# Minus mu enters the second attention's sigmoid through three more rows of the score product, not through ScalarE's bias operand

## What is computed

```
scores = jnp.einsum('bhqd,bhkd->bhqk', q, k) / scale
scores = jax.nn.sigmoid(scores - mu) * jnp.exp(scores)
scores = scores / jnp.sum(scores, axis=-1, keepdims=True)
out = jnp.einsum('bhqk,bhkd->bhqd', scores, v)
```

## Time and profile before

| what | value |
|---|---|
| median of 3 runs | 779.44 us (777.09, 779.44, 789.72) |
| profiled execution, first to last instruction | 779.1 us |
| PE busy | 707.4 us (91%) |
| DVE busy | 442.6 us (57%) |
| ACT busy | 357.8 us (46%) |
| POOL busy | 129.2 us (17%) |

### The profile page before, as it was taken

The page is one execution under the profiler, slowest core; times in us unless marked ns, Lnnn a source line. Parts: engine busy times, 40 slices in busy tenths (PEclk is TensorE's granted clock), DMA queues, the critical chain, the costliest instruction groups (busy, mean ns, idle before and its releaser), DMA issues.

```text
span 779.1 us, 16167 instructions
## 1 busy us (share of the span) xinstructions
PE 707.4 (91%) x5688; PEld 580.0 (74%) x5696; DVE 442.6 (57%) x1125; ACT 357.8 (46%) x610; POOL 129.2 (17%) x166
## 2 busy tenths in 40 slices
PE   5687999999989999999999999998899999998635
PEld 4466878878768999999999999996566665665423
DVE  3557688888673342344222232332788898866666
ACT  3242454345533212122212112213998989988435
POOL 2010122232132210000001001002634222210000
PEclk9699999999999999999999999999999999999855
DMA  6979166355737566555555555571875447651002
GB/s 172 213 133 262 31 97 102 79 86 87 121 109 268 189 209 223 189 192 172 180 189 181 199 192 177 169 180 46 101 113 95 67 63 104 82 65 18 1 14 95
DMA packets 70839, 102.54 MB, mean 132 GB/s; under 512 B 8416, under 2 KB 58600, under 8 KB 70640
## 3 DMA queue, kind: packets, MB, share of 16 engines
q1 hardware_dynamic: 67376, 93.15, 50.7%
q0 software_dynamic: 3136, 8.40, 4.2%
q10 hardware_dynamic: 256, 0.07, 0.0%
HBM read 63.75 MB, written 12.58 MB: 98 GB/s over the span
## 4 chain that ended last, share of the span: by engine, by line
PE 61%; DVE 17%; ACT 7%; DMA 7%; issue 5%; POOL 1%; SPq 1%; ACTq 1%; DVEq 0%; POOLq 0%
PE psum L1981 18%; PE psum L2032 17%; DVE arena L1304 9%; DMA arena<-arena 5%; PE psum L1661 4%; PE psum L1924 3%; PE psum L1685 2%; PE psum L1930 2%; ACT arena L830 2%; PE psum L1939 1%; POOL w0T L699 1%; PE psum L2009 1%; DVE arena L1157 1%; PE psum L2149 1%; PE psum L1654 1%
## 5 line engine op out<-in xcount | busy, mean ns | idle before, releaser
L1981 PEld LDWEIGHTS psum<-arena 128*128 128x128 f32 x1248 | 144.9, 192 | 2.1 <-issue 0.3
L1981 PE MATMUL psum<-arena 128*128 128x128 f32 x1248 | 146.1, 275 | 0.1
L2032 PE MATMUL psum<-arena 128*128 x624 | 141.4, 380 | 0.8 <-DVE arena L1450 0.8
L859 ACT ACTIVATE arena<-psum,arena 128x128 f32<-128x128 f32 x156 | 44.5, 368 | 194.7 <-PE psum L1981 115.2
L2032 PEld LDWEIGHTS psum<-arena 128*128 128x128 f32 x624 | 115.5, 190 | 15.4 <-issue 1.2
L1432 DVE TENSOR_SCALAR arena<-psum,arena 128x128 f32<-128x128 f32 x156 | 44.0, 345 | 80.5 <-PE psum L1981 67.3
L1939 PE MATMUL psum<-arena 96*128 96x256 bf16 x512 | 75.1, 274 | 9.1 <-ACT arena L829 5.7
L1304 DVE TENSOR_TENSOR arena<-arena 128x1024 f32<-128x1024 f32 x64 | 79.9, 1316 | 4.5 <-ACT arena L829 2.6
L1939 PEld LDWEIGHTS psum<-arena 96*128 96x128 bf16 x512 | 44.3, 97 | 44.0 <-ACT arena L829 14.4
L699 POOL DMA_INDIRECT w0T<-yg,pos x32 | 37.4, 1169 | 222.6 <-DMA yg<-arena 176.2
L1450 DVE TENSOR_TENSOR arena<-psum,arena 128x256 f32<-128x256 f32 x39 | 16.6, 425 | 96.6 <-PE psum L2032 96.6
(11 more groups left out here) (290 smaller groups left out, 1207.8 us busy)
## 6 DMA issues: line engine op xcount, KB each, us to landing
arena<-in_L_ffn_w_dram SPq DMA_DIRECT2D x47, 1024.0 KB, 5.1
arena<-arena SPq DMA_DIRECT2D x192, 128.0 KB, 5.1
arena<-xg SPq DMA_DIRECT2D x39, 128.0 KB, 2.0
yg<-arena SPq DMA_DIRECT2D x39, 128.0 KB, 1.7
out_dram<-arena SPq DMA_DIRECT2D x8, 256.0 KB, 2.1
xg<-zeros SPq DMA_DIRECT2D x9, 128.0 KB, 2.9
arena<-in_x_dram SPq DMA_DIRECT2D x8, 128.0 KB, 3.1
arena<-in_L_ffn_b_dram SPq DMA_DIRECT2D x1, 1024.0 KB, 14.9
```

The costliest lines, as they stand in the source:

```text
L859: ins = act.activation(hidT[:, v, c, :], psum[:, 2 * v, c * P:(c + 1) * P], ACT.Relu, bias=b1c[:, v, c:c + 1])
L1981: mm = pe.matmul(psum[:, 2 * v + c // HALF, (c % HALF) * P:(c % HALF + 1) * P], w1b[:, i % W1_BUFS, d, c * P:(c + 1) * P], xtT[:, v, d, :] ...
L2032: mm = pe.matmul(y_bank, hidT[:, u, c, :], w2s[:, one(e), c, :].rearrange("p o n -> p (o n)"), start=(c == 0), stop=(c == HC - 1))
```

## The change

The sigmoid loses its bias operand. In its place the score product of the sigmoid's pass contracts over 99 rows (`MU_ROWS`): rows 96 to 98 of `stackq1` hold ones, the same rows of `stackk1` hold minus mu, split into three bf16 parts whose sum is the fp32 value. The exp's pass still contracts over 96 rows. To fill those rows:

- DVE splits `neg_mu` and sets each part in its partition, with seven instructions on 128 x 1 values, behind the output of MoE tile 7 (`mu_parts`).
- POOL writes ones and then minus mu's parts into partitions 96 to 127 of the first copies, two instructions on 32 x 4096 bf16 values, once the first layer of MoE tile 9 is done.
- SP copies the three rows to the second copies with two DMAs of 24 KB each after the last tile is stored (`mu_rows_copied`); PE waits for them before batch 1.

```diff
-                    return act.activation(out, in_, ACT.Sigmoid, bias=neg_mu[:])
+                    return act.activation(out, in_, ACT.Sigmoid)
...
-                def scores(b, u, p, done):
+                def scores(b, u, p, done, rows):
...
-                                           stackk1[u][0:ROWS, hd, kt * P:(kt + 1) * P], stackq1[u][0:ROWS, hd, :],
+                                           stackk1[u][0:rows, hd, kt * P:(kt + 1) * P], stackq1[u][0:rows, hd, :],
...
+                                pe.wait_ge(S["consts"], ROW_CONSTS + 2)
+                            if b == 1 and p == 0:
+                                pe.wait_ge(S["w_in"], LATE_LOADS + 2 * 16)
...
-                            scores(b, u, p, S["s1_mm"])
+                            scores(b, u, p, S["s1_mm"], (ROWS, MU_ROWS)[u])
...
-                            scores(b, u, p, S["s2_mm"])
+                            scores(b, u, p, S["s2_mm"], (ROWS, MU_ROWS)[v])
...
+                pool.wait_ge(S["l1_hi"], EARLY_TILES + 2)
+                pool.memset(stackq1[0][ROWS:P], 1.0).then_inc(S["consts"], 1)
+                pool.wait_ge(S["consts"], ROW_CONSTS + 1)
+                pool.wait_ge(S["p_const"], MU_STEPS)
+                pool.tensor_scalar(stackk1[0][ROWS:P], stackq1[0][ROWS:P], mu_r[ROWS:P, 2:3], None, ALU.mult
+                                   ).then_inc(S["consts"], 1)
+                pool.wait_ge(S["consts"], ROW_CONSTS + 2)
...
+                def mu_rows_copied():
+
+                    sp.wait_ge(S["l2_mm"], MOE_TILES)
+                    sp.wait_ge(S["y_ev"], MOE_TILES)
+                    for u in range(2):
+                        sp.wait_ge(y_st[u], 16 * ((MOE_TILES + 1 - u) // 2))
+                    sp.wait_ge(S["consts"], ROW_CONSTS + 2)
+                    for stack in (stackq1, stackk1):
+                        sp.dma_start(stack[1][ROWS:MU_ROWS], stack[0][ROWS:MU_ROWS]).then_inc(S["w_in"], 16)
...
+                    if i == 7:
+                        mu_parts()
```

More of the change, by code:

```diff
@@ L67 @@
 SHIFT_ROW = ROWS
+MU_PARTS = 3
+MU_ROWS = ROWS + MU_PARTS
 Q_SLOTS = ((0, 1, 2), (3, 4), (5,))
@@ L124, in tower_kernel @@
         neg_mu = sb("neg_mu", [P, 1], F32)
+        mu_p = sb("mu_p", [P, 2], BF16)
+        mu_r = sb("mu_r", [P, 3], F32)
         ones_row = sb("ones_row", [1, P], F32)
@@ L399, in tower_kernel @@
         WT_STEPS = 10
+        CONST_STEPS = 7
+        MU_STEPS = CONST_STEPS + 7
+        ROW_CONSTS = 15
         PLAN_STEPS = 22
@@ L596, in _ @@
                 moe_tiles(tile)
+                def mu_rows_copied():
[6 more added lines that the diff above has]
+                        sp.dma_start(stack[1][ROWS:MU_ROWS], stack[0][ROWS:MU_ROWS]).then_inc(S["w_in"], 16)
                 def iteration(b, u, k):
+                    if b == 0:
+                        mu_rows_copied()
                     if stages(b + 1, 0, LAST):
@@ L1420, in weight_rounded, with mu_link, mu_parts @@
                     assert steps[0] == W8_STEPS
+                mu_steps = [CONST_STEPS]
+                def mu_link(ins):
+                    mu_steps[0] += 1
+                    ins.then_inc(S["p_const"], 1)
+                    dve.wait_ge(S["p_const"], mu_steps[0])
+                def mu_parts():
+                    dve.wait_ge(S["wT_done"], WT_STEPS + 3)
+                    mu_link(dve.tensor_copy(mu_p[:, 0:1], neg_mu[:]))
+                    mu_link(dve.tensor_tensor(mu_r[:, 0:1], neg_mu[:], mu_p[:, 0:1], ALU.subtract))
+                    mu_link(dve.tensor_copy(mu_p[:, 1:2], mu_r[:, 0:1]))
+                    mu_link(dve.tensor_tensor(mu_r[:, 1:2], mu_r[:, 0:1], mu_p[:, 1:2], ALU.subtract))
+                    mu_link(dve.tensor_tensor(mu_r[:, 2:3], mu_p[:, 0:1], ident[:, ROWS:ROWS + 1], ALU.mult))
+                    mu_link(dve.scalar_tensor_tensor(out=mu_r[:, 2:3], in0=mu_p[:, 1:2], scalar=ident[:, ROWS + 1:ROWS + 2],
+                                                     in1=mu_r[:, 2:3], op0=ALU.mult, op1=ALU.add))
+                    mu_link(dve.scalar_tensor_tensor(out=mu_r[:, 2:3], in0=mu_r[:, 1:2], scalar=ident[:, ROWS + 2:ROWS + 3],
+                                                     in1=mu_r[:, 2:3], op0=ALU.mult, op1=ALU.add))
+                    assert mu_steps[0] == MU_STEPS
                 def tile(i, u):
```

## The result

| | median | lowest to highest | runs |
|---|---|---|---|
| before | 782.39 us | 777.09 to 789.72 | 6 |
| after | 793.94 us | 787.72 to 794.98 | 6 |

The ratio is 1.0116 with an interval of 1.0082 to 1.0151, so the change costs 9.1 us (6.4 to 11.8) of 782.4. The two medians of the table stand further apart, 11.6 us or 1.48%; the text goes by the ratio, which has the interval. The forecast was 0.7 us less, 778.7 us with a range of 775.6 to 781.4, made on the 779.44 us of the three runs of before that were known then. The profiled execution of the changed kernel took 794.69 us, its span 792.9.

The account below looks back on a forecast made before the run. The second attention was taken as bound by a chain of waits through DVE's multiplications, PE and ACT, with one sigmoid per batch on it. 8 x 0.09 = 0.72 us saved, other parts 0, gave 778.7 us, range 775.6 to 781.4.

Parts of the forecast that it names:

- Two POOL instructions of 32 x 4096: MoE stage near 317 us: memset 5 us and multiplication 7 us, covered by over 100 us; cost 0 unless DVE suffers.
- third rival: MoE stage: POOL's long instructions hold DVE, which holds PE beyond 3 us slack; 783.4 us, at most 790; chance 0.05.
- The bias operand: Second attention: dropping it saves 0.09 us per sigmoid, one per batch on the path, 0.72 us in all.
- eight-fold sum of 0.7 us: Second attention: 8 x 0.09 = 0.72 us saved, one sigmoid on the path in each batch.
- The 99 rows: Second attention's score matmuls: three more rows cost 0; with scatter, 0.2 us in all either way.
- The seven DVE instructions: Behind MoE tile 7's output: cost 0, covered by PE's matmuls; without that cover at most 2.8 us.
- SP's copies and PE's waits: Copies in SP's 8.9 us gap before the spread at 543.74 us, waits covered: cost 0, at most 1.3 us.
- fourth rival: End of second attention, 730 to 745 us: PE's clock steps at another moment, 3 us either way, 776 or 782; chance 0.08.

Follow-up runs that it names:

- f2: Changed kernel with POOL's long multiplication left as it was and DVE's copy of b1 written as a maximum over a one-element axis: 787.13 us, ratio 0.999 to before.
- e4: Kernel before with the sigmoid's bias operand dropped and nothing in its place, minus mu left out of the computation: 787.28 us, ratio 1.0009 to before.
- e1: Changed kernel with POOL's multiplication made by one ACT instruction at tile 9, POOL keeping the memset: 786.93 us, ratio 1.0013 to before.
- e2: Changed kernel with POOL's multiplication split into 16 instructions of 32 x 256, one per head: 789.27 us, ratio 1.0023 to before.
- f4: Changed kernel with POOL's multiplication split into two instructions of 32 x 2048: 787.84 us, ratio 1.0013 to before.
- e3: Kernel before, bias and 96 rows kept, plus only the seven small DVE instructions and POOL's two long ones: 795.44 us, ratio 1.0115 to before.
- f3: Kernel before plus the seven DVE instructions and POOL's two, the multiplication over 32 x 8192 in one instruction: 807.29 us, ratio 1.0239 to before.
- f1: Kernel before, unchanged, profiled again on the chip of the later runs: 782.43 us in a single execution.

## Why the prediction was wrong

**The step that failed** is "Two POOL instructions of 32 x 4096 ... Cost 0, unless DVE suffers". It covered POOL's own queue, with over 100 us to spare, and that was right; the clause at its end was the whole result. It failed in four places.

- *The length.* "I take 5 for the memset and 7 for the other, nearer to the first row, since both have at most one tensor input." The memset took 3.51 us, the multiplication 10.64, which is 2.6 ns for each element of a partition and near the tensor_tensor row (3.4 ns), not the memset's. The bounds of 4.9 to 14 held for the second and not for the first.
- *The start.* "near 317 us: one tile ... before 324.41" is a tile too late. PE makes first layers two tiles ahead of the second layers, and tile 9's is this one in the trace of before, which ends at 309.75 (after, the memset starts at 315.35, as the first layer that starts at 311.55 ends):

```profile
306.02 3.73 PE L1981 MATMUL psum<-arena 128*128 128x128 f32 x32
```

  That POOL is seen at 315.35 and 318.96, near the forecast, is luck: tile 7's second layer, too, lay 5.5 us later in that run (308.09 for 302.56). And with the prediction's own figures POOL ends at 317 + 5 + 7 = 329, so by its own sum the condition of its third rival, POOL still at work at 328.60, was met; it had a chance of 0.05 all the same.
- *Who is held.* The third rival, at a chance of 0.05, had the mechanism and its slack: a DVE instruction held for over 3 us, the rest lost to PE; the measured cover is 3.6. But it took the fp8 weight's rounding for the instruction that could be held, and put the chance low since that comes late in the tile and "nearly all of DVE's work in a tile reads from PSUM". The one exception mattered: the 0.17 us copy of b1, which is in every tile, stands ahead of both relus, and fell 2 us into POOL's instruction. At 0.17 us it is in no row that the prediction cites.
- *The price.* 7 - 3 = 4 us; it was 4.86 of pause, and 1.55 more after it, for which the rival had no term. With the measured length the pause would have come out near: 8.44 of extra hold less 3 is 5.4.

The rule on ports that the third rival cites stands up to the trace. The Trainium skill, "SBUF — State Buffer", section "Who interferes with whom", says that copies and tensor_scalars can use the pair of ports shared with GpSimd, if their operands meet its conditions, that whoever issues first then has it for its whole instruction, and that a tensor_reduce on trn2 never contends. By that the copy can be held and the reduction cannot; after and f2 show 8.61 and 0.17 us. With the same section in hand, the question for the trace would have been which DVE instructions of a tile are copies or tensor_scalars, not which are long.

**The steps that held.**

- *The bias operand*: 1033 ns in after, 1032 in e4, against 1123. The chain of waits in the last full period of the changed kernel reads as worked out:

```profile
682.26 0.48 ACT w0T L948
...
686.74 1.15 ACT L855
...
689.09 10.26 DVE arena L1330 x8
...
706.75 0.49 ACT w0T L948
...
711.23 1.15 ACT L856
...
713.58 9.96 DVE arena L1330 x8
```

  Copy to table load is 4.48 us where pass 1 is sigmoid (682.26 to 686.74) and where it is exp (706.75 to 711.23); the period is 24.49 us (689.09 to 713.58), the forecast to the hundredth. That period is 24.49 or 24.50 us in all six traces without the operand (after, e1, e2, e4, f2, f4) and 24.57 or 24.58 in all four with it (the two of before, e3, f3). The four periods ahead of it, in which gathers run, range from 24.4 to 25.1 us with the operand and without it, and the first one is even longer without it (25.71 to 26.59 us in six traces, against 25.05 to 25.52 in four). So the eight-fold sum of 0.7 us is not seen in any run: from the second group of multiplications to the eighth it is 145.07 us (590.66 to 735.73) after and 145.04 before. The size is shown for the quiet period; for the sum it is only argued.
- *The 99 rows*: with shapes kept apart, a matmul over 99 rows takes 274 ns in the mean after; those over 96 rows in the same attention took 274 before and take 280 after.
- *The seven DVE instructions*: they stand between 312.20 and 313.64 us. Second layers start at 308.09, 315.34 and 322.69, 7.25 and 7.35 us apart.
- *SP's copies and PE's waits*: e1 and f2 keep them and stand at 1.0013 and 0.999. The DMA queue of SP in the changed kernel has the two copies in the gap between the last stores and the spread, as forecast, and they are done 6.3 us ahead of it; the spread takes 8.72 us for the 8.09 of the earlier trace rows:

```profile
542.02 4.88 SPq L591 DMA_DIRECT2D yg<-arena  x2
548.39 1.61 SPq L614 DMA_DIRECT2D arena<-arena  x2
556.29 8.72 SPq L571 DMA_DIRECT2D arena<-arena  x12
```

**What stays open.** The hold accounts for 6.6 us of 9.1. In the traces nothing else costs in the MoE stage: from the second layer of tile 7 to that of the last tile it is 227.59 us in all seven traces without a hold (before, f1, e1, e2, e4, f2, f4), and 234.16, 234.32 and 244.55 in after, e3 and f3, which is 6.6, 6.7 and 17.0 more. The ratios of these three give 9.1, 9.0 and 18.8 us. The excess of 1.8 to 2.5 us lies within each interval (6.4 to 11.8 for the change) but is on the same side three times, and no experiment shows another cost.

A part of it may lie at the border to the second attention. From the last tile's second layer to the first multiplication it is 20.12 us in e2, e4, f2 and f4, 21.89 in both traces of before, and 22.70, 23.01 and 22.80 in after, e3 and f3; but it is 22.75 in e1 as well, which has no hold. PE's clock goes with it. This is the view of stretches over the 15 us that begin 5 us behind the start of that second layer, in e4, before, after and e1:

```profile
543.32:558.32 15.00, 11.11 (x69) 8.54 (x70) 6.09 (x15) 13.27 (x19) 4.09 (x5) 1.00 0.64 106
```

```profile
535.16:550.16 15.00, 12.06 (x67) 9.46 (x68) 4.63 (x10) 11.71 (x17) 3.90 (x4) 0.89 0.51 92
```

```profile
547.25:562.25 15.00, 12.48 (x60) 9.37 (x61) 3.83 (x9) 10.94 (x16) 3.90 (x4) 0.77 0.47 91
```

```profile
544.11:559.11 15.00, 12.48 (x59) 9.33 (x60) 3.77 (x9) 10.88 (x16) 3.90 (x4) 0.77 0.47 91
```

The end of the kernel moves in the same way. From the last batch's first multiplication to the end it is 57.01 us in before and 54.14 in f1, which is the same kernel; in the 8 us that begin 12 us behind that multiplication PE's mean granted clock is 0.50 in the one and 1.00 in the other. That is the prediction's fourth rival, with its 3 us, in an unchanged kernel. The trace of the changed kernel has 57.15 there, so the rival has no part in its distance from before. What sets the clock's moment at either place was not tried.

The profiled spans differ by more, 13.8 us (792.9 - 779.1). The second layer that starts at 324.41 us in the earlier trace rows starts at 336.50 after, 12.1 us later: 6.6 are the hold, and 5.5 were there two tiles before it, at the second layer of 308.09 (302.56 in before), ahead of the first instruction that the change adds (312.20). Code that the change does not touch differs by as much between runs: that layer starts at 302.56 and 305.67 us in the two traces of before and at 310.72 in e4. What makes the periods with gathers move by half a microsecond from run to run was not tried.

## What to carry to other kernels

Work on an idle engine is free only if no short instruction on a critical path can be held by it: before a long GpSimd instruction is put beside a tuned stage, list VectorE's copies in that stage, however short, and ask who waits for each. Keep each GpSimd instruction shorter than the slack behind those copies (here 3.6 us; 16 pieces of 1 us were safe, while two halves of 5.5 us were enough only because the copy came 2.1 us into the first), or write the copy in a form that isn't held (a reduction over one element), or give the work to another engine. And a shorter instruction on a 93% busy engine is worth what the chain of waits gives it, here one sigmoid of the eight in a batch.

## What the runs showed of the hardware that was not expected

- POOL's multiplication by a value per partition took 10.64 us for 32 x 4096 bf16 elements and 21.00 us for 8192 columns, 2.6 ns a column; its memset of the same size took 3.51 us, 0.86 ns a column. ACT made the same product in 3.79 us.
- A copy of eight values per partition took 18.98 us beside POOL's instruction of 21.00, while a reduction of the same values, and DVE's work on 128 x 1 values, ran at their usual 0.15 to 0.17 us beside it. The first two steps of the fp8 weight's rounding, tensor_scalars on 128 x 512 values in SBUF, took 0.65 and 0.50 us beside POOL's pieces in e2, against 0.48 and 0.43 after. The memset, at 315.35 to 318.86, held nothing that the trace shows, but no copy lay beside it.
- PE's clock pays for the pause. The same view of stretches, of the changed kernel, across the second layer before the pause, the pause, the matmuls behind it and the next layer:

```profile
323.00:326.00 3.00, 3.00 (x16) 2.57 (x14) 3.00 (x1) 0.00 (x0) 3.00 (x1) 1.00 0.85 321
326.30:331.10 4.80, 0.01 (x1) 0.00 (x0) 4.76 (x7) 1.41 (x5) 3.30 (x1) 0.97 0.02 8
331.20:336.40 5.20, 5.20 (x34) 5.20 (x35) 0.93 (x6) 1.14 (x4) 0.00 (x0) 0.71 0.52 154
336.60:340.00 3.40, 3.40 (x18) 2.99 (x17) 1.07 (x4) 0.37 (x1) 0.00 (x0) 1.00 0.31 128
```

  The mean granted clock is 0.71 in the stretch behind the pause, part of it at 1.2 GHz, and back at 1.00 (2.4 GHz) 5 us later. That is the 1.55 us that a short hold adds to its own length.
